# A state-space layer, cross attention and an FFN on one core: the state matmuls move to the end of the next slot, and the prologue is dealt out anew

## What is computed

```python
# layer 1, a Mamba-2 block: 128 heads of 64 channels, 8 groups of 16 heads, state width 128
h = x * rsqrt(mean(x*x) + eps) * norm_w
proj = einsum('bsd,od->bso', h, in_proj_w)          # gate 8192, hidden 8192, B and C 1024 each, dt 128
hBC = silu(causal_conv(hBC, conv_w, conv_b))        # 4 taps along the tokens
dt = softplus(dt + dt_bias); A = -exp(A_log)
# per head: y_i = sum over j <= i of (C_i . B_j) * exp(cs_i - cs_j) * hid_j * dt_j,  cs = cumsum(A * dt)
y = y + Dp * hid
yg = y * silu(gate)
out = residual + einsum(rmsnorm_per_group(yg) * gnorm_w, out_proj_w)
# layer 2: both operands rounded to 8 bits, matmul with ctx (512 x 512 a batch)
# layer 3: x @ W.T + b plus a small expert term
```

## Time and profile before

| | |
|---|---|
| median of 3 runs | 836.12 us (833.25 to 836.18) |
| profiled execution | 831.96 us, its span 830.2 us |
| TensorE busy | 791.9 us, 95% of the span |
| TensorE weight loads | 609.6 us |
| VectorE busy | 621.9 us, 75% |
| ScalarE busy | 600.0 us, 72% |
| GpSimd busy | 623.6 us, 75% |
| mean granted TensorE clock | 0.988 |

### The profile page before, as it was taken

One profiled execution on the slowest core, in us unless ns is written; L12 is line 12 of the kernel. 1 busy time (PEld: TensorE's weight loads), 2 busy tenths in 40 slices (PEclk: granted clock), 3 DMA queues, 4 the chain that ended last, 5 costly groups with the idle time before them and its releaser, 6 DMA issues.

```text
span 830.2 us, 13187 instructions
## 1 busy us (share of the span) xinstructions
PE 791.9 (95%) x4267; PEld 609.6 (73%) x4270; DVE 621.9 (75%) x752; ACT 600.0 (72%) x1047; POOL 623.6 (75%) x561
## 2 busy tenths in 40 slices
PE   6699899999999999999999999999999999989997
PEld 4566677777777777777777777777777777767664
DVE  7768878868677867778686876777786877788774
ACT  2578586888768777888678877888588876887442
POOL 6497774789857995789767986789677986786231
PEclk9889899999999999999999999999999999999999
DMA  7343232333143342433253333324243324330001
GB/s 283 128 152 120 72 128 90 128 128 127 64 156 126 124 127 94 145 103 128 67 185 127 96 120 135 124 93 155 79 159 123 119 78 153 128 125 29 3 2 51
DMA packets 48811, 94.92 MB, mean 114 GB/s; under 512 B 3952, under 2 KB 36848, under 8 KB 48784
## 3 DMA queue, kind: packets, MB, share of 16 engines
q1 hardware_dynamic: 48784, 94.58, 34.6%
HBM read 93.26 MB, written 1.31 MB: 114 GB/s over the span
## 4 chain that ended last, share of the span: by engine, by line
PE 60%; DVE 18%; ACT 11%; issue 8%; DMA 1%; POOL 1%; ACTq 0%; DVEq 0%; SPq 0%
PE ps_z L1075 18%; PE ps_out L1181 15%; PE ps_h L1075 12%; PE ps_y L1168 7%; DVE conv_bc L716 4%; ACT decay L519 4%; DVE conv L716 4%; PE ps_t L1053 2%; ACT L519 2%; ACT conv L467 2%; DVE yg L839 2%; DVE v L833 2%; ACT conv_bc L451 1%; DVE decay L774 1%; DVE y_lo L845 1%
## 5 line engine op out<-in xcount | busy, mean ns | idle before, releaser
L716 DVE SCALAR_TENSOR_TENSOR conv<-ps_h,w_raw,conv 128x510 f32<-128x510 f32 (+2 forms) x192 | 143.3, 746 | 102.1 <-ACT conv L467 97.5
L519 ACT ACTIVATE decay<-csx,cs_own 128x256 f32<-128x256 f32 (+1 forms) x512 | 184.4, 443 | 3.5 <-POOL csx L345 2.5
L307 POOL TENSOR_TENSOR win_lo<-w_raw,win_hi 128x1024 fp32r<-128x1024 f32 x64 | 153.0, 2391 | 0.0
L402 POOL TENSOR_TENSOR sqacc<-sqacc,sq 128x512 f32<-128x512 f32 x47 | 69.5, 1479 | 109.1 <-ACT sq L555 109.1
L774 DVE TENSOR_TENSOR decay<-decay,cbm 128x1536 f32<-128x1536 f32 x64 | 125.1, 1954 | 4.4 <-ACT decay L519 4.4
L527 ACT ACTIVATE hidT<-conv 128x512 f32<-128x512 f32 x64 | 40.5, 633 | 100.9 <-DVE conv L716 100.9
L1168 PE MATMUL ps_y<-decay,hid_dt 128*64 128x256 f32 (+1 forms) x1024 | 99.0, 336 | 12.4 <-DVE hid_dt L822 12.2
L1168 PEld LDWEIGHTS ps_y<-decay,hid_dt 128*64 128x64 f32 x1024 | 64.2, 138 | 55.7 <-issue 19.6
L345 POOL TENSOR_SCALAR_AFFINE_SELECT csx<-csx 128x512 f32<-128x512 f32 x128 | 103.8, 837 | 0.0
L1181 PE MATMUL ps_out<-wout_hi,y_lo 128*128 128x512 f32 x252 | 99.9, 397 | 0.0
L1181 PE MATMUL ps_out<-wout_lo,y_hi 128*128 128x512 f32 x252 | 99.5, 395 | 0.0
(11 more groups left out here) (315 smaller groups left out, 1490.5 us busy)
## 6 DMA issues: line engine op xcount, KB each, us to landing
w_raw<-in_wmain SPq DMA_DIRECT2D x64, 772.0 KB, 4.4
csx<-cs_rows SPq DMA_DIRECT2D x128, 256.0 KB, 3.5
bc_raw<-in_wbc SPq DMA_DIRECT2D x8, 517.0 KB, 3.6
ctx_raw<-in_ctx SPq DMA_DIRECT2D x1, 2048.0 KB, 14.2
acc<-in_x SPq DMA_DIRECT2D x4, 256.0 KB, 3.0
bc_raw<-in_wffn SPq DMA_DIRECT2D x2, 512.0 KB, 3.8
out_x<-acc SPq DMA_DIRECT2D x4, 256.0 KB, 2.1
csx<-in_wdt SPq DMA_DIRECT2D x1, 256.0 KB, 4.1
```

Source lines behind the costliest of these rows:

```text
L307: eng.tensor_tensor(win_lo[:, r2, :], w_raw[:, r4, 0:W_IN], win_hi[:, r2, :].bitcast(f32), ALU.subtract).then_inc(low_win, 1)
L402: eng.tensor_tensor(sqacc[:], sqacc[:], sq[:, (k - 1) % 2, :], ALU.add).then_inc(pool_sq, 1)
L519: done = eng.activation(decay[:, r2, b, h, lo:lo + n], csx[:, r2, b, h, lo:lo + n], ACT.Exp, bias=cs_own[:, r2, t, h:h + 1])
L716: eng.scalar_tensor_tensor(out=out_b[:, :, back:], in0=src_b[:, :, 0:S - back], scalar=w[:, TAPS - 1 - back:TAPS - back], in1=out_b[:, :, ...
```

## The change

Two parts. **In the slots**: TensorE does the state matmuls of pair s-1 at the end of slot s, directly behind the transposes of pair s (in slots 0 and 1 of a group ahead of them); in slots 0 and 7 `project_out` stands ahead of the gate projection. ScalarE takes `decays` of pair s in slot s, in two halves around `finish_y`, which now belongs to pair s-2, and `tap`, `hidden` and `gates` follow. VectorE does `combine` and `lower_y` of pair s-2, the mask of pair s-1, and the convolution last. One more pair is left to finish behind the last slot. **In the prologue**: TensorE starts with 92 small matmuls (`EARLY`) on a tile that VectorE fills; x is loaded from two queues; ScalarE splits the first B, C and hidden weights and normalises half of the tiles; the residual is one GpSimd instruction a tile in place of one on VectorE and one on GpSimd; softplus is cut differently; w_raw of pairs 2 and 3 is loaded early; the causal mask of `cbm` goes (`csx` is masked already).

```diff
@@ TensorE
-            eng.wait_ge(pre_pool, 9)
-            keep_up(ps_t, WARM_UP)
+            eng.wait_ge(pre_dve, 1)
+            for _ in range(EARLY):
+                mm(ps_y[:, 0:P], onesb[:], onesb[:], start=True, stop=True)
...
                 project(ps_h[:], win_hi[:, r2, 0:KT * P], win_lo[:, r2, 0:KT * P], pe_hid)
-                if not (first and k == 0):
+                if turned and not (first and k == 0):
+                    project_out(s, g, k)
...
+                project(ps_z[:], win_hi[:, r2, KT * P:], win_lo[:, r2, KT * P:], pe_gate)
+                if not turned and not (first and k < 2):
+                    project_out(s, g, k)
+                if k == 0:
+                    products_of_bc(s, g)
+                if k == 1 and not first:
+                    sum_channels(s, g - 1)
+                if k < 2 and not (first and k == 0):
                     scan_heads(s, k)
...
                 done.then_inc(pe_tr, 1)
+                if k >= 2:
+                    scan_heads(s, k)
@@ ScalarE
+            for t in range(1, TT, 2):
+                eng.dma_start(acc[:, t, :], x_d[t // 2, (t % 2) * P:(t % 2 + 1) * P, :]).then_inc(x_in[t], 16)
             eng.wait_ge(wdt_in, 16)
             eng.activation(wdt_hi, wdt, ACT.Copy).then_inc(pre_act, 1)
+            eng.wait_ge(bc_in, 16)
+            eng.activation(wbc_hi[:], bc_raw[:, 0:BC_W], ACT.Copy).then_inc(hi_wbc, 1)
+            for t in range(1, TT, 2):
+                eng.wait_ge(pre_dve, DVE_NMR)
+                eng.activation(normed[:, t, :], acc[:, t, :], ACT.Identity, bias=resid[:, 2, t:t + 1],
+                               scale=lnr[:, 0, t:t + 1]).then_inc(pre_act, 1)
+            eng.wait_ge(w_in[0], 16)
+            eng.activation(win_hi[:, 0, :], w_raw[:, 0, 0:W_IN], ACT.Copy).then_inc(hi_win, 1)
...
+                decays(s, k, 0)
+                finish_y(s, g, k, first)
+                decays(s, k, 1)
...
                 tap(s, g, k)
-                hidden(s, k)
-                gates(s, k)
-                finish_y(s, g, k, first)
-                if not (last and k == PPG - 1):
-                    decays(s + 1, k + 1)
...
+                hidden(s, k)
+                gates(s, k)
@@ VectorE
             def slot(eng, s, g, k, first, last):
-                r2 = k % 2
+                if not (first and k < 2):
+                    combine(s, k)
                 if not (first and k == 0):
                     scale_hidden(s, k)
                 if k == 2 and not first:
                     add_group(g - 1)
+                if not (first and k == 0):
+                    mask(s, g, k)
+                if not (first and k < 2):
+                    lower_y(s, k)
...
+                conv_hidden(s, k)
@@ GpSimd, prologue
             for t in range(TT):
-                eng.wait_ge(pre_dve, DVE_HT + t + 1)
-                eng.tensor_tensor(acc[:, t, :], acc[:, t, :], residual[t], ALU.add).then_inc(pre_pool, 1)
+                eng.wait_ge(pre_dve, DVE_RES)
+                eng.wait_ge(pre_pe, KT)
+                eng.tensor_scalar(acc[:, t, :], acc[:, t, :], resid[:, 0, t:t + 1], resid[:, 1, t:t + 1], ALU.mult,
+                                  ALU.add).then_inc(pre_pool, 1)
```

More of the change, by code:

```diff
@@ L33 @@
 WARM_UP = 40
+EARLY = 92
 NEVER = -3.0e38
@@ L215, in _ @@
         def _(eng):
-            for t in range(TT):
+            for t in range(0, TT, 2):
                 eng.dma_start(acc[:, t, :], x_d[t // 2, (t % 2) * P:(t % 2 + 1) * P, :]).then_inc(x_in[t], 16)
@@ L236, in slot @@
                 r = k % 4
-                if not (first and k < 2):
+                if not (first and k < 4):
                     if late(s - 3):
@@ L507, in slot, with decays @@
                     scale_context(PPG - 1)
-            def decays(s, k):
-                r2 = k % 2
-                eng.wait_ge(pool_own, s + 1)
-                eng.wait_ge(pool_sel, 2 * s + 2)
-                if late(s - 1):
-                    eng.wait_ge(pe_y, s - 1)
-                for b in range(B):
+                if k == PPG - 1 and not last:
+                    silu_bc(0, g + 1, conv_bc[:])
+                if k == 0:
+                    silu_bc(1, g, conv_bc[:])
+                hidden(s, k)
+                gates(s, k)
+            def decays(s, k, part=None):
+                r2 = k % 2
+                if part != 1:
+                    eng.wait_ge(pool_own, s + 1)
+                    eng.wait_ge(pool_sel, 2 * s + 2)
+                    if late(s - 1):
+                        eng.wait_ge(pe_y, s - 1)
+                for b in range(B) if part is None else (part,):
                     for h in range(2):
@@ L781, in slot, with mask @@
                     quantise_context(k - 2)
+                if first and k == PPG - 1:
+                    eng.wait_ge(pre_pool, POOL_RSTD + TT)
                 if last and k in (4, 5):
                     quantise_context(k + 2)
+            def mask(s, g, k):
+                eng.wait_ge(act_exp, s)
+                if k == 1:
+                    eng.wait_ge(dve_cb, 2 * g + 2)
+                q2 = (k - 1) % 2
+                eng.tensor_tensor(decay[:, q2], decay[:, q2], cbm[:].unsqueeze(2).broadcast_to([P, B, 2, MJ]),
+                                  ALU.mult).then_inc(dve_m, 1)
             def conv_hidden(s, k):
```

327 lines of the change are left out of this document (165 added, 162 removed).

## The result

The changed kernel takes 924.3 us (median of 4 runs, 923.0 to 927.3), the one before 835.2 on the same chip (4 runs, 833.3 to 836.2): a ratio of 1.108, 95% interval 1.104 to 1.111. It is slower, as forecast, but by 89 us in place of 26, and outside the range.

A forecast was written before the change was run, and what follows sets the result against it. The prediction took TensorE, working 95% of the span, as the bound. Its terms summed to +26.3 us on the profiled 832.0, so 858.3, and 2 more gave 860 us; range 828 to 890.

The forecast's parts named there:

- The circle: Slots 3 to 6: state matmuls, Exp, tap, convolution, Silu, transposes close a loop of 11.28 us against 10.46; +26.2 us.
- the first rival: ScalarE's table load goes out ahead of the wait, so the loop doesn't close; 826 or 814 us, chance 0.20.
- the ring: Another name for the circle: the 11.28 us loop through TensorE and ScalarE, 0.82 us a slot over the matmuls.
- VectorE reaches the convolution sooner: Slots 3 to 6: VectorE's work ahead of the convolution sums to 5.8 us, less 0.3 overlap, against 6.27 for the tap.
- the blocked rival: VectorE and GpSimd block each other in the loop; slot 11.8 us, 890 us in all, chance 0.22.
- the main case: The forecast itself, 860 us with its own range of 846 to 872, chance 0.52.
- Slots 7 and 0: +0.6 a group: The extra convolution delays the gate projection and hidT by 0.4 and 0.2 us a group; +5.0 us with last slot 7.
- Slot 2: add_group ahead of the mask makes VectorE the later one; 12.7 us in place of 10.46, +16.9 us over 7 groups.
- Stalls gone: Late decay no longer holds TensorE: -10.6 us in group 0, -5.0 us in the last group and the loop.
- Tail: Behind the last slot, one more pair is left to finish; +3.0 us.
- Prologue: Softplus begins at 17.1 and slot 2 of group 0 at 43.7; -9.2 us, between -5 and -13.
- Neighbourhood of the state matmuls: Placing them behind transposes could save 0 to 0.3 us a pair, 19 us at most; taken as 0.

The follow-up runs named there:

- gpsimd_light_after: Changed kernel with all four GpSimd weight-splitting instructions (high and low parts) cut to 64 columns from pair 4 on; 857.5 us, ratio 1.027.
- gpsimd_lo_light: Changed kernel with only GpSimd's two low-weight instructions (win_lo, wout_lo) cut to 64 columns from pair 4 on; 848.8 us, ratio 1.017.
- the experiment: The changed prologue with the slots of the kernel before; 826.6 us, ratio 0.990 to the kernel before.

## Why the forecast was right in kind and wrong in size

- **The circle** (11.28 us a slot): right. 11.23 in slot 5, 11.24 in all of slots 3 to 5 once GpSimd's low weights are out. Its premise on the wait at the table load held: the load starts 0.16 us behind T in the row (388.15), so the first rival, in which it goes out ahead of the wait, fell. Opened by hand the ring gives 31 us against gpsimd_light_after, part of it slot 4's, and 23 against gpsimd_lo_light; the forecast's terms for it were 26.2 and part of 5.0.
- **The failed step** is the sentence "VectorE reaches the convolution sooner", 5.8 us out of `yg` 0.87, mask 1.95 and `y_lo` 1.42. These were durations of the order before, where VectorE did the three behind the convolution. In the slot of the earlier trace rows `win_lo` ran while VectorE waited for the tap and did the convolution, to 355.19:

```profile
352.81 2.38 POOL L307 TENSOR_TENSOR win_lo<-w_raw,win_hi 128x1024 fp32r<-128x1024 f32 x1
```

  In the new order the same three are 1.23, 2.85 and 1.27 us on average, and in the slot shown the convolution starts at T + 6.96. This is the blocked rival, and its 11.8 us are what slots 3 and 4 show (11.84, 12.27). It was given 0.22 where the main case had 0.52; the three means were taken into the main sum as if they were properties of the instructions, though the rival had already said what they would meet in the new order.
- **What no case priced** is where TensorE meets the delay. All cases let it wait at the transposes alone. `project_out` of pair s-2 now needs the `y_lo` of the same slot, due at about T + 5.8, or T + 2.9 in slots 7 and 0: 65.6 us of waits in the rows above, against 2.1. "Slots 7 and 0: +0.6 a group" measured +3.8 (13.22 to 14.63, 12.09 to 14.48), and slots 1 and 6, put at 0 and 0.8, +1.5 and +2.2. In gpsimd_lo_light they are +0.3 (7 and 0 together), -0.2 and +0.8, as forecast. That is why 890 was too low as an upper end, too.
- **Slot 2**, +2.3 a group: measured 1.95, and 1.4 to 1.6 without the low weights; the lower bound was the better value.
- **Stalls gone**, -15.6: group 0 from slot 2 on is 1.6 us longer, not 6 shorter, since the new waits fill the space. In gpsimd_lo_light it is 4.0 shorter (77.83 to 73.86).
- **Tail** with the last slot: +3.7, forecast 3.8, and that is luck. Pair 63's state matmuls stand 13.6 us behind the last slot's start in place of 11.5, so the order costs 2.1. Most of the rest stands in the last layer, which the change doesn't touch: from 910 to 916 us the granted clock is 0.72, where the kernel before has 1.00 at that stage.
- **Prologue**: -7.7 at slot 2, -8.8 in the experiment, forecast -9.2. Softplus begins at 15.86, sooner than the 17.1 forecast, but a clock dip stays (the hidden projection of slot 1 takes 2.05 us for four matmuls in place of 1.10, at a granted clock of 0.50 from 33.8 to 36.8 us).
- **Neighbourhood of the state matmuls**, taken as 0: right to 0.1 us. In the row of gpsimd_lo_light transposes and state matmuls take 2.04 us up to the next slot, 1.98 forecast.
- With the low weights out of the way the kernel takes 849 to 858, the forecast was 860, its steady group 98.3 against 96.6 to 98.0. Of the 13.7 us a steady group 1.4 are the order alone (92.42 to 93.84), and the rest is the ring and GpSimd: 2.8 and 9.5 by way of gpsimd_lo_light (96.63), 4.1 and 8.1 by way of gpsimd_light_after (97.98).
- Trainium skill, "ScalarE: Activation LUTs", section "What ACT_TABLE_LOAD costs", and its drain of 1.38 us on top of each load: no run here shows it. From load to Exp it is 1.30 us in every slot looked at (358.90 to 360.20 in gpsimd_lo_light), and the ring closes with that number.

## What to carry over

An instruction's mean duration belongs to its place in the order: when work of VectorE that meets GpSimd moves from a slack place onto a ring, price it at the blocked duration (here its shortest time, plus what is left of the GpSimd instruction that will be running, less 0.14 us for the mask), and ask of every consumer, not only of the ring's, when it now needs the result. A shift by one slot that takes a stage out of TensorE's middle can pay nothing when TensorE has no wait to lose there; look first for the wait it would remove. Before touching the order, look at what stands beside the stalls that there are: moving a few small roundings gave 5.5 us between medians.
